# Every loop of the five engines' programs written out as straight-line code

## The chip, the cores and the metric

The kernel runs on one core of a Trainium2 chip. The metric is the device time of one execution in microseconds (us); lower is better. The kernel before takes 1512.36 us, the median of three runs (1511.91 to 1512.64).

## The reference, cut to what matters

The input is `x` (32 x 64 tokens of 256 numbers) with a context of the same shape. Two cross-attention layers with 16 heads of 128 come first, then an MLP, then a third attention with 16 small heads, then another MLP. All is float32.

```python
def _cross_attention(q_in, kv_in, wq, bq, wk, bk, wv, bv, wo, bo, bias_k, bias_v):
    qh = (q_in @ wq + bq).reshape(b, q_len, H, K)          # H, K = 16, 128
    kh = (kv_in @ wk + bk).reshape(b, t, H, K)             # and one bias key per head
    vh = (kv_in @ wv + bv).reshape(b, t, H, K)
    weights = softmax(einsum('bqhk,bthk->bhqt', qh, kh) / sqrt(K))
    return einsum('bhqt,bthk->bqhk', weights, vh).reshape(b, q_len, H * K) @ wo + bo

x = x + cross_attention(layer_norm(x), ctx)    # layer 1
x = x + cross_attention(layer_norm(x), ctx)    # layer 2
x = x + gelu(layer_norm(x) @ w_fc1 + b_fc1) @ w_fc2 + b_fc2
# then: 16 heads of 16, keys from ctx (masked) and x, residual, RMS norm, and a second MLP
```

## The kernel before, in words

Each of the five engines has its own program, and semaphores tie them together. Float32 products are made of three products of split numbers (a high part and a low part), which the helper `three` issues (lines 168 to 170). So almost all matmul rows carry these three line numbers.

**The two cross-attention layers** fill most of the time. A layer is 32 units: 8 pairs of heads by 4 groups of 512 tokens. In one slot an engine works on the front of one unit (queries, keys, values, logits) and on the back of the unit before it (probabilities by values, and the output projection with `WHI` and `CHI`). The logits of a unit are the matmuls of line 413. `slots` (line 241) calls `slot` once for the first unit, then runs a loop (`Fori`, line 248) whose body holds 8 slots and that runs three times, and then writes the last 8 slots out. Around that stands the loop over the two layers (line 466 on PE, 538 on ACT, 660 on DVE, 306 on POOL). POOL has an inner loop of its own over pairs of weights (line 309), and SP one over the weight loads (line 273).

**The two MLPs** (`mlp`, tags m0 and m1) go over four groups of tokens. The first group is written out and the other three are one loop (`groups`, line 686).

**The third attention** is 64 steps in a software pipeline, two for each batch. `steps` writes the first 9 out, then runs a loop of four steps a turn, 13 turns (line 1024), and then writes the rest. A step on PE is four logits matmuls (line 1066), one mask matmul (1070), four transposes (1080) and eight products with the values (1092); every other step has one more transpose (1101).

An induction variable of `Fori` lives in a register. Addresses are given as `bass.ds(2 * m, 2)`, and the wait values, `e.wait_ge(q_done, 2 * n + h + 1)` say, are worked out by register instructions on the engine that waits. At its end a loop has one register addition and one compare and branch on each engine. A `Block` ends with a barrier, and its beginning is an unconditional branch.

Of the kernel before, what the change touches and what calls it, by code (L numbers as in the profile page):

```python
# [20 lines left out]
NL = 2  # L21
# [23 lines left out]
def program(nc, x, ctx_in, mask, wall, vech, vecm, b_fc2, qw, kw, vw, ow, out_b, w1, w2, b2, out):  # L45
    es = ExitStack()
    with es:
# [139 lines left out]
        with ExitStack() as ph:  # L187
# [54 lines left out]
            def slots(e, L, slot):  # L242

                slot(L, L * UNITS, 0, L * HP, None, False)
                with e.Fori(0, UNITS // OLD - 1) as i:
                    for u in range(OLD):
                        slot(L, L * UNITS + i * OLD + u + 1, u + 1, L * HP + i * 2 + (u + 1) // G, i * 2 + u // G, False)  # L250
                i = UNITS // OLD - 1
                for u in range(OLD):
                    slot(L, L * UNITS + i * OLD + u + 1, u + 1,
                         L * HP + i * 2 + (u + 1) // G if u < OLD - 1 else None, i * 2 + u // G, True)

            with nc.Block() as block:
                @block.sync
                def _(e):
                    def load(m, a):
                        e.dma_start(W[a][:, :, :, :], wall[m].rearrange("j (c p) n -> p j c n", p=P)).then_inc(w_in[a], 16)  # L260

                    ct, xt = (v.rearrange("(t p) d -> p t d", p=P) for v in (ctx_in, x))
                    for g in range(G):
                        ts = slice(g * GT, (g + 1) * GT)
                        if g >= 2:

                            e.wait_ge(ctx_turned, (g - 1) * DC)
                        e.dma_start(cin[g % 2][:, :, :], ct[:, ts, :]).then_inc(ctx_in_g[g], 16)
                        e.dma_start(X[:, ts, :], xt[:, ts, :]).then_inc(x_in[g], 16)
                        if g == 0:  # L270
                            load(0, 0)
                    load(1, 1)
                    with e.Fori(1, SETS // 2) as i:
                        for a in range(2):
                            m = i * 2

                            e.wait_ge(w_split, m + a - 1)
                            e.wait_ge(bw_done, m + a - 1)
                            load(m + a, a)

                @block.gpsimd
                def _(e):
                    e.memset(one, 1.0).then_inc(ident_one, 1)
                    e.wait_ge(ident_one, 1)
                    e.affine_select(out=ident[:, :], in_=one, compare_op=ALU.is_equal, fill=0.0, base=0,
                                    pattern=[[-1, P]], channel_multiplier=1).then_inc(ident_done, 1)
                    e.memset(EA[:, :, :], 0.0)
                    e.memset(EB[:, :, :], 0.0).then_inc(e_made, 1)
                    e.memset(PTB[:, :, :], 1.0)
                    e.memset(PRT[:, :, :], 0.0).then_inc(zeros_set, 1)  # L290

                    def split(m, a):

                        e.wait_ge(w_hi, m + 1)
                        for j in range(4):
                            i = e.tensor_tensor(WLO[a][:, j, :, :], W[a][:, j, :, :],  # L296
                                                WHI[a][:, j, :, :].bitcast(F32), ALU.subtract)
                        e.tensor_tensor(E2[a][:, :, :], EA[:, bass.ds(2 * m, 2), :], EB[:, bass.ds(2 * m, 2), :],
                                        ALU.subtract)
                        e.tensor_copy(PB[a][:, :, :], PH[:, :, bass.ds(2 * m, 2)]).then_inc(w_split, 1)  # L300

                    e.wait_ge(e_made, 3)
                    split(0, 0)
                    for g in range(G - 1):
                        norm_lo(e, norm, 0, g)
                    with e.Fori(0, NL) as L:
                        norm_lo(e, norm, L, G - 1)
                        split(L * HP + 1, 1)
                        with e.Fori(0, HP // 2 - 1) as i:
                            for a in range(2):  # L310
                                split(L * HP + i * 2 + 2 + a, a)
                        split(L * HP + HP, 0)
                        for g in range(G - 1):
                            norm_lo(e, norm, L + 1, g)

                @block.tensor
                def _(e):
# [145 lines left out]
                            norm_turn(e, norm, 0, k, PROJ[2:])  # L463

                    e.wait_ge(ctx_lo, G * DC)
                    with e.Fori(0, NL) as L:
                        slots(e, L, slot)

                @block.scalar
                def _(e):  # L470
# [64 lines left out]
                    norm_sqrt(e, norm, 0, 2)  # L535
                    norm_scale(e, norm, 0, 1, PROJ[2:])
                    norm_scale(e, norm, 0, 2, PROJ[2:])
                    with e.Fori(0, NL) as L:
                        slots(e, L, slot)

                @block.vector
                def _(e):
                    logit = logits[:, :, 0:GT * KEYS].rearrange("p h (t k) -> p h t k", k=KEYS)

                    def slot(L, n, at, pair, hp, last):
# [8 lines left out]
                        if back:  # L554
# [2 lines left out]
                            e.wait_ge(sm_done, n)  # L557
                            e.reciprocal(ri[:, :], sm[:, :]).then_inc(ri_done, 1)
                            e.wait_ge(ri_done, n)
                            e.tensor_tensor(PTB[:, gb * GT:(gb + 1) * GT, bass.ds(2 * hp, 2)].rearrange("p t h -> p h t"),  # L560
                                            ex[:, :, S].rearrange("p (h t) -> p h t", h=2),
                                            ri[:, :].rearrange("p (h t) -> p h t", h=2), ALU.mult)
                            e.tensor_tensor(PR[:, :, :], ex[:, :, 0:S], ri[:, :].unsqueeze(2).to_broadcast([P, 2 * GT, S]),
# [9 lines left out]
                        if bridge and gb == 0:  # L573
                            e.wait_ge(bw_turned, L + 1)
                            e.tensor_copy(BW[:, :], PROJ[3][0:32, 0:D]).then_inc(bw_out, 1)

                            e.tensor_copy(CUR[:, :], PM[:, bass.ds((L + 1) * LNP, 4)]).then_inc(cur_set, 1)
                        if norm_now is not None and front:

                            e.wait_ge(x_settled, 2 * n if back else 2 * n + 2)  # L580
# [76 lines left out]
                            round_set(0, 0)  # L657
                    e.wait_ge(x_in[G - 1], 16)
                    e.memset(mx[:, :], 0.0).then_inc(x_settled, 2)
                    with e.Fori(0, NL) as L:  # L660
                        e.memset(BWT[:, :, :], 0.0).then_inc(bwt_sum, 1)
                        e.wait_ge(bwt_sum, L * BWTN + 1)
                        e.tensor_copy(BWT[:, :, H + 1], PM[:, bass.ds(L * LNP + 4, 2)]).then_inc(bwt_sum, 1)
                        slots(e, L, slot)


# [3 lines left out]
        def mlp(tag, norm, k, b1, w, ready, b2d, func, dst, more):  # L670
# [3 lines left out]
            with ExitStack() as ph:  # L674
# [8 lines left out]
                def groups(e, body, tail=None):  # L683

                    body(0, True)
                    with e.Fori(1, G) as g:
                        body(g, False)
                    if tail is not None:
                        tail()

                with nc.Block() as block:  # L691
# [13 lines left out]
                    def _(e):  # L705
                        def body(g, first):
                            for j in range(FC):
# [8 lines left out]
                                    more["gpsimd"](e)  # L716
                                if j == 3:

                                    xs = X[:, bass.ds(g * GT, GT), :]
                                    e.tensor_tensor(xs, xs, b2b[:, :].unsqueeze(1).to_broadcast([P, GT, D]),  # L720
                                                    ALU.add).then_inc(b2_added, 1)

# [22 lines left out]
                    def _(e):  # L745
                        def add(g):

                            e.wait_ge(b2_added, g + 1)
                            e.wait_ge(down_used, FC * (g + 1))  # L749
                            for j in range(2):  # L750
                                xs = X[:, bass.ds(g * GT + 2 * j, 2), :]
                                e.tensor_tensor(xs, xs, bank[3 + j][:, :].rearrange("p (t n) -> p t n", n=256),  # L752
                                                ALU.add).then_inc(y_added, 1)

# [21 lines left out]
                    def _(e):  # L776
# [12 lines left out]
                            i.then_inc(down_used, 1)  # L789

                        def body(g, first):
                            toks = bass.ds(g * GTOK, GTOK)
# [68 lines left out]
        with ExitStack() as l1:  # L861
# [136 lines left out]
            with ExitStack() as ph:  # L998
# [20 lines left out]
                def steps(e, slot):  # L1019

                    for s in range(LR + 1):
                        slot(s, s, 0)
                    rest = (STEPS - LR - 1) // 4
                    with e.Fori(0, rest) as i:
                        for r in range(LR + 1, LR + 5):
                            slot(i * 4 + r, r, i * 2)
                    for s in range(LR + 1 + rest * 4, STEPS + LR):
                        slot(s, s, 0)
# [4 lines left out]
                with nc.Block() as block:  # L1033
                    @block.gpsimd
                    def _(e):
                        def slot(s, r, b0):
                            if runs(r, 0):
# [5 lines left out]
                                q = QL[:, r % 2, bass.ds((b0 + other) * S, S)]  # L1043
                                e.tensor_tensor(QE[r % 4][:, :, :], q.unsqueeze(1).to_broadcast([P, GH, S]),
                                                HM[:, :].unsqueeze(2).to_broadcast([P, GH, S]),
                                                ALU.mult).then_inc(qe_set, 1)
                            if runs(r, LR) and (r - LR) % 2 == 0:
                                b = b0 + (r - LR) // 2
                                e.wait_ge(ao_hi, b + 1)
                                toks = bass.ds(b * S, S)  # L1050
# [88 lines left out]
                    def _(e):  # L1139
                        def slot(s, r, b0):  # L1140
# [23 lines left out]
                            if runs(r, LA) and (r - LA) % 2 == 0:  # L1164
                                b, c = b0 + (r - LA) // 2, (r - LA) // 2 % 2
                                e.wait_ge(at_out, 2 * b + 2)
                                e.tensor_copy(SRC_HI[:, 1, :, bass.ds(b * S, S)], AT[c][:, :, :]).then_inc(ao_hi, 1)


                        e.wait_ge(ow_in, 16)  # L1170
# [160 lines left out]
```

## Time and profile before

| | |
|---|---|
| median of three runs | 1512.36 us |
| the three runs | 1511.91 to 1512.64 us |
| span of the profiled execution, first to last instruction | 1511.0 us |
| TensorE (PE) matmuls busy | 1426.2 us, 94% |
| weight loads (PEld) | 1274.8 us, 84% |
| VectorE (DVE) | 895.5 us, 59% |
| ScalarE (ACT) | 626.1 us, 41% |
| GpSimd (POOL) | 340.7 us, 23% |
| mean granted TensorE clock | 0.966 |
| instructions | 29462 |

The profile has no device time of the profiled execution beside its span; the median of the runs lies 1.36 us above that span, which is what surrounds the first and the last instruction. A row that names a releaser says what ended the idle time before an instruction; "issue" there means that the engine waited for nothing that the profile shows. Rows with a q behind the engine are its sequencer's (register instructions, branches, waits). PE and PEld are issued by one sequencer.

### The profile page before, as it was taken

What the parts mean: (1) busy time and instruction counts of PE and PEld (TensorE: products, weight loads), DVE (VectorE), ACT (ScalarE), POOL (GpSimd) and SP (SyncE); (2) the same over time, 40 slices, a digit from 0 to 9 for tenths busy, and PEclk for the clock granted to TensorE, in tenths of its full rate; (3) what the DMA queues carried; (4) which work ended last, traced back from release to release, by engine and by line L of the source; (5) the groups of instructions that cost most, each with busy time, mean ns of one, the idle gap of its engine ahead of it and who ended that gap; (6) DMA issues with size and microseconds to landing.
All of it is one profiled execution on the core that took longest, in us unless ns stands there. A gap on an engine that the chain in (4) does not pass through costs nothing. (4 is left out here: it accounts for less than half of the span.)

```text
span 1511.0 us, 29462 instructions
## 1 busy us (share of the span) xinstructions
PE 1426.2 (94%) x11575; PEld 1274.8 (84%) x11575; DVE 895.5 (59%) x1929; ACT 626.1 (41%) x1053; POOL 340.7 (23%) x322
## 2 busy tenths in 40 slices
PE   4999999999999899999999999998898999997898
PEld 3899899899998778988998999986787888887787
DVE  6566567566666646666665666665523377776422
ACT  4533344334333543433343344343422336666521
POOL 4201101101011111101101011020754035555654
PEclk8999999999999979999999999997899999999899
DMA  5000000000000000000000000000000000001000
GB/s 169 29 29 1 30 5 25 30 1 29 29 2 29 1 30 1 29 29 1 29 1 30 29 1 29 29 1 1 25 0 8 0 1 1 0 0 60 4 28 28
DMA packets 28991, 30.42 MB, mean 20 GB/s; under 512 B 651, under 2 KB 28883, under 8 KB 28883
## 3 DMA queue, kind: packets, MB, share of 16 engines
q1 hardware_dynamic: 28658, 28.72, 6.0%
q8 instruction: 88, 1.44, 0.4%
q14 instruction: 19, 0.16, 0.0%
q10 hardware_dynamic: 226, 0.10, 0.0%
HBM read 26.72 MB, written 2.10 MB: 19 GB/s over the span
## 5 line engine op out<-in xcount | busy, mean ns | idle before, releaser
L296 POOL TENSOR_TENSOR WLO<-W,WHI 128x512 fp32r<-128x512 f32 x68 | 85.1, 1283 | 793.5 <-DVE WHI L623 793.5
L168 PE MATMUL bank<-SRC_HI,WHI 128*128 128x512 f32 (+1 forms) x576 | 233.4, 405 | 18.5 <-issue 14.6
L169 PE MATMUL bank<-SRC_LO,WHI 128*128 128x512 f32 (+1 forms) x576 | 231.9, 403 | 0.0
L170 PE MATMUL bank<-SRC_HI,WLO 128*128 128x512 f32 (+1 forms) x576 | 231.5, 402 | 0.0
L570 DVE STREAM_TRANSPOSE PRT<-PR 32x256 f32<-32x256 f32 x512 | 223.3, 436 | 8.4
L591 DVE TENSOR_TENSOR CLO<-bank,CHI 128x512 fp32r<-128x512 f32 x128 | 88.2, 691 | 159.3 <-ACT CHI L502 159.1
L478 ACT ACTIVATE QT<-bank,PB 128x512 f32<-128x512 f32 x128 | 88.2, 690 | 209.2 <-PE bank L170 209.2
L168 PE MATMUL bank<-WHI,CHI 128*128 128x256 f32 x512 | 155.2, 303 | 0.0
L168 PE MATMUL bank<-WHI,SRC_HI 128*128 128x256 f32 x512 | 149.4, 292 | 0.0
L168 PEld LDWEIGHTS bank<-SRC_HI,WHI 128*128 128x128 f32 x576 | 111.2, 193 | 42.7 <-issue 15.4
L170 PE MATMUL bank<-WHI,CLO 128*128 128x256 f32 x512 | 145.6, 284 | 0.0
L169 PE MATMUL bank<-WLO,CHI 128*128 128x256 f32 x512 | 145.6, 284 | 0.0
L169 PE MATMUL bank<-WLO,SRC_HI 128*128 128x256 f32 x512 | 143.9, 281 | 0.0
L170 PE MATMUL bank<-WHI,SRC_LO 128*128 128x256 f32 x512 | 143.9, 281 | 0.0
L617 DVE TENSOR_TENSOR X<-X,bank 128x512 f32<-128x512 f32 x128 | 88.0, 688 | 85.9 <-PE bank L170 85.9
L385 PE MATMUL bank<-PRT,V 128*128 128x128 f32 x1024 | 128.3, 280 | 7.8 <-issue 6.0
L170 PEld LDWEIGHTS bank<-SRC_HI,WLO 128*128 128x128 f32 x576 | 110.8, 192 | 26.9
L169 PEld LDWEIGHTS bank<-SRC_LO,WHI 128*128 128x128 f32 x576 | 111.4, 193 | 22.6
L385 PEld LDWEIGHTS bank<-PRT,V 128*128 128x128 f32 x1024 | 122.8, 196 | 8.7 <-issue 6.5
L482 ACT ACTIVATE KT<-bank,PB 128x512 f32<-128x512 f32 x128 | 88.4, 691 | 91.7 <-PE bank L170 91.7
L486 ACT ACTIVATE V<-bank 128x512 f32<-128x512 f32 x128 | 76.5, 597 | 97.6 <-PE bank L170 97.2
L168 PEld LDWEIGHTS bank<-WHI,CHI 128*128 128x128 f32 x512 | 98.3, 192 | 17.0 <-issue 13.2
(182 smaller groups left out, 2976.5 us busy)
## 6 DMA issues: line engine op xcount, KB each, us to landing
W<-in_wall SPq DMA_DIRECT2D x18, 1024.0 KB, 5.6
V<-in_ctx SPq DMA_DIRECT2D x4, 512.0 KB, 5.5
X<-in_x SPq DMA_DIRECT2D x4, 512.0 KB, 6.5
mlp_w<-in_w SPq DMA_DIRECT2D x2, 1024.0 KB, 7.4
out<-X SPq DMA_DIRECT2D x4, 512.0 KB, 3.0
W<-in_qw SPq DMA_DIRECT2D x1, 256.0 KB, 3.9
W<-in_kw SPq DMA_DIRECT2D x1, 256.0 KB, 4.1
W<-in_vw SPq DMA_DIRECT2D x1, 256.0 KB, 4.9
```

Source lines behind the costliest of these rows:

```text
L168: e.matmul(dst, a_hi, b_hi, start=start, stop=False, **kw)
L169: e.matmul(dst, a_hi, b_lo, start=False, stop=False, **kw)
L170: return e.matmul(dst, a_lo, b_hi, start=False, stop=stop, **kw)
L296: i = e.tensor_tensor(WLO[a][:, j, :, :], W[a][:, j, :, :], WHI[a][:, j, :, :].bitcast(F32), ALU.subtract)
L385: i = e.matmul(bank[3 + h][:, p * P:(p + 1) * P], V[(at - 1) % 2][:, p, h * K:(h + 1) * K], PRT[:, h * GT + p, :], start=True, stop=True)
L478: e.activation(QT[:, h, :], PROJ[h][:, :], ACT.Identity, bias=PB[a][:, 0, h:h + 1]).then_inc(q_out, 1)
L482: e.activation(KT[:, h, :, 0:S], PROJ[2 + h][:, :].rearrange("p (q k) -> p q k", k=S), ACT.Identity, bias=PB[a][:, 1, h:h + 1]).then_inc(k ...
L486: e.activation(V[at % 2][:, 2 * j:2 * j + 2, :], PROJ[j][:, :].rearrange("p (t n) -> p t n", n=256), ACT.Copy).then_inc(v_out, 1)
L570: i = e.transpose(PRT[b * S + z:b * S + z + 32, :, b * S + y:b * S + y + 32], PR[b * S + y:b * S + y + 32, :, z:z + 32])
L591: e.tensor_tensor(CLO[:, h, :], bank[3 + h][:, :], CHI[:, h, :].bitcast(F32), ALU.subtract).then_inc(c_lo, 1)
L617: e.tensor_tensor(xs, xs, bank[3 + j][:, :].rearrange("p (t n) -> p t n", n=256), ALU.add).then_inc(x_settled, 1)
```

## The change

Every `with e.Fori(a, b) as i:` becomes `for i in range(a, b):`, which the program builder runs, so that the body stands in the program once for each turn. Addresses by `bass.ds` become plain slices. The wait values become constants, since they are computed while the program is built. No matmul, activation, vector operation, DMA or semaphore is added, left out or put elsewhere in its engine's order.

```diff
 def slots(e, L, slot):
-    with e.Fori(0, UNITS // OLD - 1) as i:
+    for i in range(0, UNITS // OLD - 1):
         for u in range(OLD):
             slot(L, ...)
...
-    with e.Fori(1, SETS // 2) as i:               # SP, weight loads
+    for i in range(1, SETS // 2):
...
-    with e.Fori(0, NL) as L:                      # PE, ACT, DVE, POOL
+    for L in range(0, NL):
         slots(e, L, slot)
...
-    with e.Fori(0, HP // 2 - 1) as i:             # POOL, weight splits
+    for i in range(0, HP // 2 - 1):
...
-    e.tensor_copy(PB[a][:, :, :], PH[:, :, bass.ds(2 * m, 2)]).then_inc(w_split, 1)
+    e.tensor_copy(PB[a][:, :, :], PH[:, :, slice(2 * m, 2 * m + 2)]).then_inc(w_split, 1)
...
 def groups(e, body, tail=None):                   # both MLPs
     body(0, True)
-    with e.Fori(1, G) as g:
+    for g in range(1, G):
         body(g, False)
...
 def steps(e, slot):                               # third attention
-    with e.Fori(0, rest) as i:
+    for i in range(0, rest):
         for r in range(LR + 1, LR + 5):
             slot(i * 4 + r, r, i * 2)
```

On PE, at the end of the eight-slot body of the cross-attention, the program before has this (the products with `CHI` and `CLO` are the output projection of one unit; the branch leads back to the top of the body, where the products with `SRC_HI` of the next unit begin):

```order
L168 MATMUL bank<-WHI,CHI 128x256
L169 MATMUL bank<-WLO,CHI 128x256
L170 MATMUL bank<-WHI,CLO 128x256
L248 REGISTER_ALU
L248 COMPARE_AND_BRANCH
```

and the changed program has this at the same place:

```order
L168 MATMUL bank<-WHI,CHI 128x256
L169 MATMUL bank<-WLO,CHI 128x256
L170 MATMUL bank<-WHI,CLO 128x256
L168 MATMUL bank<-SRC_HI,WHI 128x512
L169 MATMUL bank<-SRC_LO,WHI 128x512
L170 MATMUL bank<-SRC_HI,WLO 128x512
```

The register instruction and the branch are gone, and the next unit's first matmul stands right behind.

On PE in the third attention, the last step of the body before (an ISA row is a register instruction that makes an address or a wait value):

```order
L1061 REGISTER_ALU
L1066 ISA
L1066 MATMUL bank<-KL,QE 128x128 x4
L1070 ISA
L1070 MATMUL bank<-MA,ONE 128x4x64
L1080 MATMUL bank<-ident,XN 128x128 x4
L1092 MATMUL bank<-VS,HT 64x17 x8
L1098 ISA
L1100 REGISTER_ALU
L1101 MATMUL logits<-ident,AN 128x128
L1024 REGISTER_ALU
L1024 COMPARE_AND_BRANCH
```

and one such step of the changed program:

```order
L1066 MATMUL bank<-KL,QE 128x128 x4
L1070 MATMUL bank<-MA,ONE 128x4x64
L1080 MATMUL bank<-ident,XN 128x128 x4
L1092 MATMUL bank<-VS,HT 64x17 x8
L1101 MATMUL logits<-ident,AN 128x128
```

The matmuls keep their order; seven register and branch rows go.

## Rows read from the trace of the kernel before

**Rows 1.** The page's first part, all engines: busy us, share, instructions
```profile
PE 1426.2 (94%) x11575; PEld 1274.8 (84%) x11575; DVE 895.5 (59%) x1929; ACT 626.1 (41%) x1053; POOL 340.7 (23%) x322
```

**Rows 2.** Waits, whole span: us in total, times, longest us
```profile
PE bank L168 <- issue: 14.6, 4, 3.7
PE bank L168 <- DVE X L752: 1.5, 6, 0.5
```

**Rows 3.** Instructions of line 248, duration ns min/median/max, first and last start us
```profile
L248 PEldq COMPARE_BRANCH  x6: 83/5410/5536, 162.6 to 919.2; - x6
```

**Rows 4.** Timeline of PE around the first turn: start us, us, what, idle before
```profile
168.39 0.49 PE L168 MATMUL bank<-SRC_HI,WHI 128*128 128x512 f32 x1 [3.67 <-issue]
169.18 0.39 PE L168 MATMUL bank<-SRC_HI,WHI 128*128 128x512 f32 x1
...
170.15 0.63 PE L168 MATMUL bank<-SRC_HI,WHI 128*128 128x512 f32 x1
```

**Rows 5.** Windows: stretch, us, busy (x) of PE, PEld, DVE, ACT, POOL; PEclk; DMA; GB/s
```profile
169.54:172.95 3.41, 3.41 (x10) 2.63 (x9) 2.59 (x5) 0.69 (x1) 0.67 (x1) 0.50 0.00 0
290.34:295.83 5.49, 5.49 (x13) 4.33 (x14) 3.77 (x7) 0.69 (x1) 1.54 (x2) 0.50 0.01 3
681.53:684.95 3.42, 3.42 (x10) 2.65 (x9) 3.20 (x6) 0.69 (x1) 0.05 (x1) 0.50 0.00 0
```

**Rows 6.** Timeline of PE, first logits matmuls of four units
```profile
160.56 0.34 PE L413 MATMUL logits<-KT,QT 128*64 128x65 f32 x4
180.38 0.34 PE L413 MATMUL logits<-KT,QT 128*64 128x65 f32 x4
405.49 0.33 PE L413 MATMUL logits<-KT,QT 128*64 128x65 f32 x3
419.84 0.28 PE L413 MATMUL logits<-KT,QT 128*64 128x65 f32 x2
```

**Rows 7.** Windows, the unit of the last two rows above
```profile
405.50:419.80 14.30, 14.30 (x121) 13.04 (x120) 10.56 (x21) 5.20 (x8) 2.74 (x3) 1.00 0.24 74
```

**Rows 8.** Instructions of line 1024, third attention's loop
```profile
L1024 PEldq COMPARE_BRANCH  x13: 76/208/232, 1257.0 to 1368.4; - x13
```

**Rows 9.** Timeline of PEld, line 1092, inside the loop; turns at 1284.9 and 1294.2
```profile
1284.52 0.55 PEld L1092 LDWEIGHTS bank<-VS,HT 128*64 128x64 f32 x16 [0.17 <-issue]
1287.11 0.55 PEld L1092 LDWEIGHTS bank<-VS,HT 128*64 128x64 f32 x16 [0.17 <-issue]
...
1293.80 0.55 PEld L1092 LDWEIGHTS bank<-VS,HT 128*64 128x64 f32 x16 [0.17 <-issue]
1296.39 0.55 PEld L1092 LDWEIGHTS bank<-VS,HT 128*64 128x64 f32 x16 [0.17 <-issue]
```

**Rows 10.** Timeline of PEld, line 1092, in the straight steps behind the loop
```profile
1370.32 0.55 PEld L1092 LDWEIGHTS bank<-VS,HT 128*64 128x64 f32 x16 [0.17 <-issue]
1372.53 0.55 PEld L1092 LDWEIGHTS bank<-VS,HT 128*64 128x64 f32 x16 [0.17 <-issue]
1374.80 0.55 PEld L1092 LDWEIGHTS bank<-VS,HT 128*64 128x64 f32 x16 [0.17 <-issue]
```

**Rows 11.** Instructions of line 686, the MLPs' loops
```profile
L686 PEldq COMPARE_BRANCH  x6: 76/210/233, 1105.2 to 1499.2; - x6
```

**Rows 12.** Instructions of line 466, the loop over layers on PE
```profile
L466 PEldq COMPARE_BRANCH  x2: 74/1754/3433, 543.5 to 1055.1; - x2
```

**Rows 13.** Waits on DVE, 545 to 551 us
```profile
DVE BWT L661 <- issue: 2.4, 1, 2.4
```

**Rows 14.** DMA queues, 168 to 288 us, one turn of the body: packets, MB
```profile
q8 instruction: 10, 0.16, 0.5%
```

**Rows 15.** DMA queues, 410 to 530 us, eight units written out
```profile
q8 instruction: 7, 0.11, 0.5%
```

**Rows 16.** DMA queues, 1258 to 1370 us, third attention's loop, the only instruction queue
```profile
q14 instruction: 1, 0.01, 0.0%
```

**Rows 17.** Windows, one turn of the third attention's loop
```profile
1294.24:1303.52 9.28, 9.22 (x126) 8.21 (x122) 7.25 (x19) 6.36 (x15) 4.96 (x6) 1.00 0.00 0
```

More of the change, by code:

```diff
@@ L297, in split @@
                                                 WHI[a][:, j, :, :].bitcast(F32), ALU.subtract)
-                        e.tensor_tensor(E2[a][:, :, :], EA[:, bass.ds(2 * m, 2), :], EB[:, bass.ds(2 * m, 2), :],
+                        e.tensor_tensor(E2[a][:, :, :], EA[:, slice(2 * m, 2 * m + 2), :], EB[:, slice(2 * m, 2 * m + 2), :],
                                         ALU.subtract)
-                        e.tensor_copy(PB[a][:, :, :], PH[:, :, bass.ds(2 * m, 2)]).then_inc(w_split, 1)
+                        e.tensor_copy(PB[a][:, :, :], PH[:, :, slice(2 * m, 2 * m + 2)]).then_inc(w_split, 1)
                     e.wait_ge(e_made, 3)
@@ L465, in _ @@
                     e.wait_ge(ctx_lo, G * DC)
-                    with e.Fori(0, NL) as L:
+                    for L in range(0, NL):
                         slots(e, L, slot)
@@ L537, in _ @@
                     norm_scale(e, norm, 0, 2, PROJ[2:])
-                    with e.Fori(0, NL) as L:
+                    for L in range(0, NL):
                         slots(e, L, slot)
@@ L559, in slot @@
                             e.wait_ge(ri_done, n)
-                            e.tensor_tensor(PTB[:, gb * GT:(gb + 1) * GT, bass.ds(2 * hp, 2)].rearrange("p t h -> p h t"),
+                            e.tensor_tensor(PTB[:, gb * GT:(gb + 1) * GT, slice(2 * hp, 2 * hp + 2)].rearrange("p t h -> p h t"),
                                             ex[:, :, S].rearrange("p (h t) -> p h t", h=2),
@@ L575, in slot @@
                             e.tensor_copy(BW[:, :], PROJ[3][0:32, 0:D]).then_inc(bw_out, 1)
-                            e.tensor_copy(CUR[:, :], PM[:, bass.ds((L + 1) * LNP, 4)]).then_inc(cur_set, 1)
+                            e.tensor_copy(CUR[:, :], PM[:, slice((L + 1) * LNP, (L + 1) * LNP + 4)]).then_inc(cur_set, 1)
                         if norm_now is not None and front:
@@ L659, in _ @@
                     e.memset(mx[:, :], 0.0).then_inc(x_settled, 2)
-                    with e.Fori(0, NL) as L:
+                    for L in range(0, NL):
                         e.memset(BWT[:, :, :], 0.0).then_inc(bwt_sum, 1)
                         e.wait_ge(bwt_sum, L * BWTN + 1)
-                        e.tensor_copy(BWT[:, :, H + 1], PM[:, bass.ds(L * LNP + 4, 2)]).then_inc(bwt_sum, 1)
+                        e.tensor_copy(BWT[:, :, H + 1], PM[:, slice(L * LNP + 4, L * LNP + 4 + 2)]).then_inc(bwt_sum, 1)
                         slots(e, L, slot)
@@ L717, in body @@
                                 if j == 3:
-                                    xs = X[:, bass.ds(g * GT, GT), :]
+                                    xs = X[:, slice(g * GT, g * GT + GT), :]
                                     e.tensor_tensor(xs, xs, b2b[:, :].unsqueeze(1).to_broadcast([P, GT, D]),
@@ L750, in add @@
                             for j in range(2):
-                                xs = X[:, bass.ds(g * GT + 2 * j, 2), :]
+                                xs = X[:, slice(g * GT + 2 * j, g * GT + 2 * j + 2), :]
                                 e.tensor_tensor(xs, xs, bank[3 + j][:, :].rearrange("p (t n) -> p t n", n=256),
@@ L791, in body @@
                         def body(g, first):
-                            toks = bass.ds(g * GTOK, GTOK)
+                            toks = slice(g * GTOK, g * GTOK + GTOK)
                             for j in range(FC):
@@ L1042, in slot @@
                                 other = r // 2 + (1 if r // 2 % 2 == 0 else -1)
-                                q = QL[:, r % 2, bass.ds((b0 + other) * S, S)]
+                                q = QL[:, r % 2, slice((b0 + other) * S, (b0 + other) * S + S)]
                                 e.tensor_tensor(QE[r % 4][:, :, :], q.unsqueeze(1).to_broadcast([P, GH, S]),
@@ L1049, in slot @@
                                 e.wait_ge(ao_hi, b + 1)
-                                toks = bass.ds(b * S, S)
+                                toks = slice(b * S, b * S + S)
                                 e.tensor_tensor(SRC_LO[:, 1, :, toks], AT[(r - LR) // 2 % 2][:, :, :],
@@ L1166, in slot @@
                                 e.wait_ge(at_out, 2 * b + 2)
-                                e.tensor_copy(SRC_HI[:, 1, :, bass.ds(b * S, S)], AT[c][:, :, :]).then_inc(ao_hi, 1)
+                                e.tensor_copy(SRC_HI[:, 1, :, slice(b * S, b * S + S)], AT[c][:, :, :]).then_inc(ao_hi, 1)
                         e.wait_ge(ow_in, 16)
```

## The prediction

> **What bounds the kernel now.** The page's first part comes first: PE is busy for 1426.2 of 1511.0 us and no other engine for more than 895.5 [rows 1]. So a microsecond counts if PE would otherwise have worked in it. The waits of PE come next, and among them one kind has no releaser at all: line 168 waits for "issue" four times, 14.6 us together [rows 2]. The reader should then ask which instruction of PE's sequencer stands there. Line 248, the branch at the end of the eight-slot body, has six executions, with a median of 5410 ns and a smallest of 83 ns [rows 3]. The body runs three times in each of two layers, so four branches are taken and two fall through: four long ones and four waits. In the timeline the first turn shows 3.67 us without a matmul, and then something that a list of waits cannot show: the 512-column matmul takes 0.39 us right behind the gap and 0.63 us from 170.15 on [rows 4]. The granted clock there is 0.50 [rows 5], the lower of the two levels, 1.2 GHz, after PE had stood still.
>
> **Part 1: the four turns of the cross-attention loop.** The gaps: 14.6 us. The low clock behind them: three windows of 3.41, 5.49 and 3.42 us with PE busy all through, at clock 0.50 [rows 5], and a fourth behind the fourth turn as long as the third, 15.7 us in all, of which half, 7.9 us, is work that the full clock would have saved. Together 22.5 us. A second reading: the unit across the first turn lasts 180.38 - 160.56 = 19.82 us from logits to logits, and the unit at the same place of the schedule, between the third body and the eight slots written out behind it, 419.84 - 405.49 = 14.35 us [rows 6]. In that unit the clock is 1.00 and PE is busy throughout [rows 7]. The difference, 5.47 us, is the 3.67 us gap and the 1.7 us of clock behind it. I take 22.5 us. What is late next? Where no branch is taken PE meets no other wait in its unit, so nothing stands behind the gap to take its place. The other engines are busy for 10.56 us or less of such a unit [rows 7]; their cover stays.
>
> Why a turn costs so much is seen in the instruction queue: 10 packets of 16 KB in one turn of the body [rows 14] and 7 in a stretch of equal length and equal work that is written out [rows 15]. The jump back asks again for code that the core no longer holds. The Trainium skill says so too (Runtime: NRT & Kernel Launch, Instruction fetch mechanics): a taken branch whose target is outside the loaded pages has to wait for a fetch. By that rule and the rows alike, these four go.
>
> **Part 2: the loop over layers.** Its taken branch holds PE's sequencer for 3433 ns [rows 12], but PE works off queued matmuls meanwhile: the four waits of rows 2 are used up by the inner turns. DVE stands idle for 2.4 us at the same place [rows 13]. I cost this part at nothing. The cover is PE's own queue and DVE's slack; at most it gives the 2.4 us of DVE.
>
> **Part 3: the third attention.** A branch takes 208 ns here [rows 8], and no 16 KB packet is fetched in the 112 us of the loop [rows 16]. Yet it shows on PE: from one step's products with the values to the next it is 1287.11 - 1284.52 = 2.59 us across a turn, and 1296.39 - 1293.80 = 2.59 us again [rows 9], while the steps written out behind the loop alternate between 2.21 and 2.27 us [rows 10]. That is 0.32 us a turn: the branch, and the register instructions after it that make the first addresses while PE's queue has run dry. Twelve turns are taken: 12 x 0.32 = 3.8 us. The ends are 0, if something else fills the place, and 12 x 0.38 = 4.6 us against the shorter step. I take 3.8, since the straight steps do the same work.
>
> A rule of the Trainium skill gives another price here (Advanced Engine Details and Errata, Control Flow Timing): about 108 ns for a compare and branch. Our trace has 208 ns for the branch and 0.32 us for the turn. An estimate by the page is 12 x 0.108 = 1.3 us for this part in place of 3.8, and the whole would come out 2.5 us higher.
>
> **Part 4: the MLPs.** The branch takes 210 ns [rows 11], behind queued matmuls; the only waits of PE near it are six for DVE's addition into X, 1.5 us in all [rows 2]. That dependency stays; DVE reaches it perhaps 50 ns sooner without register instructions. I take 0.3 us, between 0 and 1.5.
>
> **Part 5: register instructions elsewhere.** Hundreds of them go on every engine. In the units PE waits for nobody [rows 7], so they are worth nothing there. At the bridges between layers PE waits on a chain over DVE and ACT; some tens of ns at each of a handful of waits. I take 0.3 us, between 0 and 2.
>
> **What it may cost.** The third attention and the MLPs now need code fetched where they turned within held code. In the units a packet lasts 120 / 7 = 17 us [rows 15], which at 241 matmuls and weight loads in 14.3 us [rows 7] is 288 of them. A turn of the third attention has 248 [rows 17]: about 10 packets for 12 turns, and, by an estimate of one packet each, 4 or 5 for the four repeated MLP groups (two in each MLP): 15. Straight code is fetched ahead in the units without any gap on PE, so I cost this at nothing, with a bound under the rivals.
>
> **The sum.** 22.5 + 3.8 + 0.3 + 0.3 = 26.9 us off. The span goes from 1511.0 to 1484.1 us, and with the 1.36 us around it (the median stands so far above the span) the time is 1485.5 us. The low-clock windows come in steps of about 3.4 us and begin where PE has idled; everything behind 165 us moves, so the other places where the clock falls, the bridges and the changes from phase to phase, may each win or lose part of a step, half of which is time. I allow 4 us either way.
>
> **Rivals.** *The stall goes but the low clock stays.* If those windows came from something other than the gaps, power say, only 14.6 + 3.8 + 0.6 = 19.0 us go: 1493.4 us. For it: the clock falls up to 1.2 us after the gap has ended. Against: in the units with no branch it never falls. *The turn moves instead of going.* If each new packet in straight code cost what a turn costs now, 3.65 us of gap and 2 us of clock, only where code was held before, 5.6 in all, 15 x 5.6 = 84 us would come on and 26.9 go: 1569 us, slower. It decides from 26.9 / 15 = 1.8 us a packet. For it: the third attention works through its code half as fast again as the units (248 instructions in 9.28 us against 241 in 14.3) [rows 7, 17], with shorter steps to hide a fetch in. Against: the units fetch straight code all the time and show no gap [rows 7, 15]. The skill (same section as above) holds such crossings mostly hidden. *Half effect.* PE's gap shrinks but the unit behind it stumbles over something that was late under its cover (DVE's transposes at that place, 10.6 us of work in 14.35), about 1 to 1.5 us a turn, and the third attention is held by DVE at 2.3 us a step: some 7 us less gain, 1492 us. *It gives more.* The register instructions on DVE and ACT shorten the bridges by 2 us and two low-clock steps vanish: 1481 us. That the change doesn't do what it says is excluded by the order of PE's instructions, which has no such branch left.
>
> **How the numbers follow.** My forecast with its few us about it has 0.72, more gain 0.06, half effect 0.08, low clock that stays 0.08, slower by fetches 0.04, and 0.02 for next to nothing. A measurement of this kernel tells 0.2%, 3 us, from no change, so all but the last two are faster: 0.94, 0.02, 0.04. The range goes from 1480.0, the larger ends of parts 3 to 5 with some luck of the clock, to 1492.5, the smaller ends with bad luck and the half effect; it leaves out the slower rival and the low clock that stays.
>
> **What would show it.** No branch of line 248, no wait of PE's line 168 for "issue" of 3.6 us; units without a branch's gap, of 14.35 us at that place, all through both layers; granted clock 1.00 from about 36 to 500 us; steps of 2.21 and 2.27 us throughout the third attention, with some 10 packets on the instruction queue in it. I am wrong if PE has gaps at packets in straight code, if the clock falls in the middle of the units without a gap, or if some step of the third attention still lasts 2.6 us.

## The result, and the profile after

The changed kernel takes 1484.97 us, the median of four runs (1484.72 to 1485.71), against 1512.46 us for the kernel before in runs beside it: a ratio of 0.9817, with a 95% interval of 0.9803 to 0.9831. The forecast was 1485.5 us. The profiled execution has a span of 1483.9 us, 27.1 us less than before.

The page's first parts, of the changed kernel; they answer to [rows 1]:

```profile
span 1483.9 us, 27446 instructions
...
PE 1415.3 (95%) x11575; PEld 1268.7 (85%) x11575; DVE 897.6 (60%) x1929; ACT 623.5 (42%) x1053; POOL 339.5 (23%) x322
...
PEclk8999999999999989999999999997999999998899
...
q8 instruction: 92, 1.51, 0.4%
```

The counts of real work are those of before, and 2016 instructions are gone, all of them the sequencers'. PE is busy for 10.9 us less with the same 11575 matmuls. 8.1 us of that is the clock's (worked out in the table under the third attention's loop); most of the rest lies in the third attention, where the busy time falls by 3.1 us at clock 1.00 (the step rows below). The instruction queue q8 carried 92 packets; before there were 88. That is about what the prediction's counts give: four turns no longer fetch three packets each again, and 15 packets of new code come on.

The waits of PE in line 168, which answer to [rows 2], of the changed kernel (us in total, times, longest):

```profile
PE bank L168 <- PEq L1199: 4.0, 1, 4.0
PE bank L168 <- PEq L256: 3.9, 1, 3.9
PE bank L168 <- DVE Y L1244: 2.3, 1, 2.3
PE bank L168 <- DVE SRC_LO L933: 1.7, 1, 1.7
PE bank L168 <- PEq L1033: 1.7, 1, 1.7
PE bank L168 <- DVE X L752: 0.6, 1, 0.6
```

The four waits for "issue", 14.6 us, have gone, and of the six for DVE's addition into X one is left. The unit at the first turn lasted 19.82 us before [rows 6]. Its first logits matmul and that of the next unit are now at:

```profile
160.97 0.34 PE L413 MATMUL logits<-KT,QT 128*64 128x65 f32 x4
...
175.36 0.34 PE L413 MATMUL logits<-KT,QT 128*64 128x65 f32 x4
```

It lasts 14.39 us. The third attention, where [rows 9] had 2.59 us across a turn, is even at 2.21 and 2.27 us:

```profile
1254.30 0.55 PEld L1092 LDWEIGHTS bank<-VS,HT 128*64 128x64 f32 x16 [0.17 <-issue]
1256.51 0.55 PEld L1092 LDWEIGHTS bank<-VS,HT 128*64 128x64 f32 x16 [0.17 <-issue]
1258.79 0.55 PEld L1092 LDWEIGHTS bank<-VS,HT 128*64 128x64 f32 x16 [0.17 <-issue]
```

The gain of this part can be read in one view: from the first step's products with the values to the last step's, the same 1811 matmuls on PE, at clock 1.00 in both kernels (before, then changed; the columns are explained below):

```profile
1236.58:1377.43 140.85, 140.05 (x1811) 124.93 (x1811) 110.25 (x275) 97.23 (x214) 70.66 (x86) 1.00 0.00 1
1209.52:1346.62 137.10, 136.98 (x1811) 124.07 (x1811) 110.01 (x275) 95.04 (x214) 70.59 (x87) 1.00 0.01 2
```

That is 3.75 us. And the DMA queues over what was its loop, 1230 to 1338 us, now show code being fetched, where [rows 16] had no q8:

```profile
q8 instruction: 11, 0.18, 0.6%
```

Where the 27.1 us went is best read stage by stage. The windows view takes a list of stretches; here both kernels are cut at the same events (first logits of each layer, last logits of each layer, first matmul of each phase). The columns are the stretch, its length, the busy time of PE, PEld, DVE, ACT and POOL with their instructions, PEclk, DMA share, GB/s. The kernel before:

```profile
45.70:515.60 469.90, 461.74 (x3791) 416.84 (x3790) 302.64 (x633) 189.72 (x294) 48.61 (x52) 0.99 0.06 19
515.60:558.30 42.70, 35.81 (x199) 28.56 (x198) 20.01 (x60) 16.23 (x26) 5.21 (x4) 0.76 0.01 2
558.30:1027.30 469.00, 460.78 (x3793) 416.06 (x3792) 302.72 (x634) 189.77 (x294) 48.57 (x52) 0.99 0.06 19
1027.30:1063.40 36.10, 25.29 (x133) 18.87 (x132) 15.93 (x43) 11.25 (x16) 5.11 (x4) 0.68 0.00 0
...
1228.80:1381.50 152.70, 149.71 (x1888) 133.68 (x1888) 117.83 (x290) 101.72 (x225) 78.91 (x96) 0.98 0.00 1
1381.50:1412.00 30.50, 17.92 (x120) 17.10 (x121) 16.26 (x24) 18.10 (x43) 20.31 (x11) 0.84 0.23 74
```

The changed kernel:

```profile
46.30:504.20 457.90, 457.15 (x3793) 413.66 (x3792) 303.34 (x634) 189.62 (x294) 48.45 (x52) 1.00 0.06 20
504.20:545.50 41.30, 34.41 (x197) 27.79 (x196) 20.33 (x60) 16.27 (x25) 5.18 (x4) 0.79 0.00 1
545.50:1003.50 458.00, 457.26 (x3792) 413.74 (x3791) 303.29 (x634) 189.62 (x294) 48.47 (x52) 1.00 0.06 20
1003.50:1038.10 34.60, 24.23 (x133) 18.03 (x133) 15.88 (x43) 11.25 (x17) 5.11 (x4) 0.75 0.00 1
...
1203.20:1350.90 147.70, 144.53 (x1889) 130.44 (x1889) 117.54 (x290) 99.45 (x225) 78.35 (x96) 0.99 0.01 2
1350.90:1384.40 33.50, 21.24 (x120) 20.35 (x120) 14.90 (x24) 18.07 (x43) 20.21 (x11) 0.75 0.26 67
```

The two layers give 12.0 and 11.0 us, the turns. The bridge and the end of the second layer give 1.4 and 1.5 us, both with less PE busy time at a higher clock. The third attention gives 5.0 us: 3.75 for the turns, and most of the rest because its first steps were not at the low clock this time. The change of phase behind it takes 3.0 us back: PE is busy for 3.3 us more with the same 120 matmuls, at clock 0.75 instead of 0.84. The stretches not shown add up to about +0.8 us: the start, the first MLP with what lies behind it, and the last MLP.

### The profile page after: what moved, and what is told of

Its sections match the earlier page's. It is cut to its first block and busy times, and to the rows that moved or that the text cites. A ratio compares the mean times of both kernels' runs of the same rounds, so it can differ in the third digit from the quotient of the medians.

```text
span 1483.9 us, 27446 instructions
## 1 busy us (share of the span) xinstructions
PE 1415.3 (95%) x11575; PEld 1268.7 (85%) x11575; DVE 897.6 (60%) x1929; ACT 623.5 (42%) x1053; POOL 339.5 (23%) x322
## 5 line engine op out<-in xcount | busy, mean ns | idle before, releaser
L168 PE MATMUL bank<-SRC_HI,WHI 128*128 128x512 f32 x576 | 230.4, 400 | 3.9 <-PEq L256 3.9
L169 PE MATMUL bank<-SRC_LO,WHI 128*128 128x512 f32 x576 | 229.4, 398 | 0.0
L170 PE MATMUL bank<-SRC_HI,WLO 128*128 128x512 f32 x576 | 229.0, 398 | 0.0
```

Source lines behind the costliest of these rows:

```text
L168: e.matmul(dst, a_hi, b_hi, start=start, stop=False, **kw)
L169: e.matmul(dst, a_hi, b_lo, start=False, stop=False, **kw)
L170: return e.matmul(dst, a_lo, b_hi, start=False, stop=stop, **kw)
```

## The experiments

Times of kernels are medians. Each ratio is to the kernel before in runs beside it, with its 95% interval. All kernels but the changed one itself are made from the kernel before with one helper, at the end of the file so that line numbers keep:

```python
def turns(e, line, start, end):
    if STRAIGHT:                  # a condition on line and e.engine, given with each run
        yield from range(start, end)
        return
    with e.Fori(start, end) as i:
        yield i
```

Every `with e.Fori(a, b) as i:` reads `for i in turns(e, line, a, b):`. Where a loop is kept, its branch has the helper's line (1338 or 1339) in the profile.

### One loop of one engine

```diff
-    if STRAIGHT:
+    if line == 248 and e.engine == mybir.EngineType.PE:
```

> Only PE's loop of line 248 (three turns of eight slots) is written out; the loop over layers, the MLP and third-attention loops and all loops of the other engines stay. Theory (PE fetches its code again at a taken branch of that loop, and idles into the low clock): the four gaps of 3.6 us and the low clock behind them go, 22.5 us less than before, about 1490 us; units across the turn 14.35 us. Rival (the gain of the change is spread over register instructions and loops of all engines): less than half of it here, 1500 us or more.

Measured: 1488.15 us (four runs) against 1510.75 us (21 runs of before), ratio 0.9843 (0.9828 to 0.9858), 22.6 us less; the interval goes from 21.5 to 26.0 us. The units have 14.35 to 14.39 us at all four places, and line 168's wait for "issue" is gone. The forecast of 22.5 us for this part is met, and it comes from a loop of PE alone. What the trace leaves is the rest: steps of 2.57 to 2.61 us at the turns of the third attention, and the six waits for DVE's addition.

```profile
PE bank L168 <- DVE X L752: 1.3, 6, 0.3
```

### The other four engines, and PE alone

```diff
-    if STRAIGHT:
+    if e.engine != mybir.EngineType.PE:      # x2
+    if e.engine == mybir.EngineType.PE:      # x3
```

> All loops of DVE, ACT, POOL and SP are written out, PE keeps every loop. Theory: PE's gaps and low-clock windows all stay, the time is that of before within 1 us (1511 to 1513 us). Rival (DVE's turns and register instructions matter): 1509 us or less.

> All loops of PE are written out, the other engines keep theirs. Theory: practically the whole gain, 1485 to 1487 us, since the other engines' turns are off the path; at most 1.5 us above the full change, at the bridges between layers where PE waits on DVE and ACT. Rival: the gain of the full change minus the part of the others, 1490 us or more.

Measured: with every engine but PE written out 1513.36 us (ten runs), ratio 1.0009 (0.9995 to 1.0022), no gain (0.4 us above the range that I expected, 1511 to 1513). With PE alone written out 1487.21 us (four runs), ratio 0.9839 (0.9824 to 0.9854), which overlaps the interval of the full change. The first kernel's trace still has the old row:

```profile
PE bank L168 <- issue: 13.9, 4, 3.6
```

So nearly all of the gain is PE's. Turns and register instructions of DVE, ACT, POOL and SP are worth nothing that the times can show here. The traces show about 1 us of theirs, in PE's waits for DVE's addition in the MLPs: the first row is of the kernel with all but PE written out, the second of PE alone:

```profile
PE bank L168 <- DVE X L752: 0.5, 1, 0.5
PE bank L168 <- DVE X L752: 1.7, 6, 0.3
```

Five of the six waits go when DVE's program is written out and stay when only PE's is. That is the effect that part 4 of the prediction put at 0.3 us; it is 1.0 to 1.2 us in these traces. Whether the 2.2 us between the medians of PE alone and the full change are real stays open: their intervals overlap.

### The third attention's loop alone

```diff
-    if STRAIGHT:
+    if line == 1024:
```

> Only the third attention's loop (line 1024) is written out, on every engine. Theory: 12 turns of 0.32 us, 3.8 us less than before (1508.6 us), every step 2.21 or 2.27 us. By the 108 ns a page gives for a branch it would be 1.3 us. Rival (new code must be fetched and holds PE): no gain or a loss.

Measured: 1509.85 us (eleven runs) against 1510.75 us (21 runs), ratio 0.999 (0.998 to 1.0). That is 0 to 3 us less, and the forecast 3.8 us lies just outside. The medians mislead here: one execution of before differs from the next by up to 9 us (1505.85 to 1514.82), and the eleven runs had less clock (median 0.965 against 0.968). Among runs with the same mean granted clock, from 0.964 to 0.968 (one to six runs of each kernel), the kernel with this loop written out is on average 2.2 to 5.0 us shorter. The steps tell it without the clock. The stretch of 140.85 us above reads

```profile
1232.61:1369.70 137.09, 136.97 (x1811) 124.05 (x1810) 110.23 (x275) 95.17 (x214) 70.63 (x87) 1.00 0.01 2
```

with steps of 2.21 and 2.27 us at all 12 turns. The same trace bears on the spread. Its first cross-attention turn has a gap of 3.32 us and no low clock behind it (its timeline of PE, and then its window from 168 to 172 us, with PEclk third from the end); the third, of 3.31 us, has one:

```profile
168.19 0.50 PE L168 MATMUL bank<-SRC_HI,WHI 128*128 128x512 f32 x1 [3.32 <-issue]
```

```profile
168.00:172.00 4.00, 3.81 (x16) 3.12 (x17) 3.89 (x8) 1.38 (x2) 0.00 (x0) 1.00 0.02 4
```

What the clock does behind a gap is thus not fixed for a kernel. To take it out, I add up in each trace the time in which PE was busy while the clock stood at 0.50, and take half of it off the span:

| kernel | span | PE busy at 0.50 | span less half of it | against before |
|---|---|---|---|---|
| before | 1511.0 | 77.2 | 1472.4 | |
| all but PE written out | 1512.8 | 81.4 | 1472.2 | -0.2 |
| third attention's loop alone | 1504.3 | 72.1 | 1468.3 | -4.1 |
| PE's line 248 alone | 1487.2 | 61.3 | 1456.6 | -15.8 |
| PE alone | 1485.0 | 61.1 | 1454.5 | -17.9 |
| the full change | 1483.9 | 61.0 | 1453.4 | -19.0 |

These are single executions, in us, to be read to about 1 us: in the third attention's kernel the four gaps were also 0.9 us shorter (13.7 against 14.6), which is in its 4.1. The full change's 19.0 us is what the prediction's terms without the clock come to (14.6 + 3.8 + 0.3 + 0.3), and the other 8.1 us (half of 77.2 - 61.0) are the clock's. Of these, 7.9 are the four windows behind the gaps; at all other places together PE was busy at the low clock for 61.5 us before and 61.0 after.

### The loop over layers put back

```diff
-    if STRAIGHT:
+    if line not in (306, 466, 538, 660):
```

> The changed kernel with the loop over the two layers put back on PE, ACT, DVE and POOL; everything inside it stays written out. One turn is taken, over a body of some 8000 PE instructions. Theory: PE's branch waits about 3.4 us for code behind queued matmuls and DVE stands idle 2.4 us, both hidden, so the time is that of the full change, 1485 us, within 1.5 us. Rival (every taken branch back to code no longer held costs PE 5.6 us): 1490.5 us.

Measured: 1485.55 us (four runs), ratio 0.9842 (0.9818 to 0.9865), the time of the full change. The branch waits as long as before, and the time does not show it:

```profile
L1338 PEldq COMPARE_BRANCH  x2: 83/1798/3512, 530.0 to 1030.8; - x2
```

Here a long taken branch costs nothing, since PE's queue holds slow work for as long: in the 3.5 us of this branch PE is busy all through, with 13 matmuls at clock 0.50.

### Gaps without a branch

```diff
+    if n % 32 in (8, 16):                       # DVE, behind its addition into X
+        for c in range(4):                      # x7; range(7) in x9
+            e.wait_ge(held, 4 * (2 * L + n % 32 // 8 - 1) + c)
+            e.tensor_copy(scr, ident broadcast to 128x512).then_inc(held, 1)
...
+    if n % 32 in (9, 17):                       # PE, ahead of the queries
+        e.wait_ge(held, 4 * (2 * L + n % 32 // 8))
```

In x9 the 4 in both waits is a 7 too. The copies write a tile that nobody reads.

> The changed kernel, no loop anywhere, but at the four places of the former turns DVE makes four idle copies behind its addition into X and PE waits for the last before the next unit's queries: four gaps on PE of 2.5 to 4 us without any branch. Theory (the low clock follows the idle time, whatever its cause): low-clock windows of one or two steps of 3.4 us behind most of the gaps, and each lengthened unit is longer by its gap and half of its low-clock time; with gaps of 3.5 us the time is 1484.97 + 14 + 7 = 1506 us, and at least 10 us above the changed kernel. Rival (the low clock came with the jump or the code fetch): only the gaps, clock 1.00 behind them, 1499 us.

> As the kernel with four gaps, but with seven copies of 0.46 us in place of four, so that PE's gaps grow from 2.50 us to about 3.9 us, as long as those before the change. Theory (whether the low clock comes depends on how long PE stood still, and 2.5 us is mostly too short): low clock behind at least three of the four gaps, 1484.97 + 15.5 + 5 to 9 us = 1505 to 1509 us. Rival (the low clock is a matter of the jump or of fetching code, and the one window at 2.5 us was an accident): clock 1.00 behind all four, 1500.5 us.

Measured with four copies: 1495.93 us (four runs), ratio to before 0.9916 (0.9888 to 0.9945), 11.0 us over the full change's median. The wait of PE, and then windows behind each of the four gaps:

```profile
PE bank L168 <- DVE scr L625: 10.0, 4, 2.5
```

```profile
168.00:180.00 12.00, 12.00 (x102) 10.74 (x101) 8.04 (x16) 5.16 (x8) 5.41 (x6) 1.00 0.01 1
287.00:289.84 2.84, 2.84 (x7) 2.26 (x8) 2.71 (x8) 0.00 (x0) 0.00 (x0) 0.50 0.00 0
674.00:686.00 12.00, 12.00 (x103) 10.75 (x102) 8.03 (x16) 5.15 (x8) 5.41 (x6) 1.00 0.01 1
793.00:805.00 12.00, 12.00 (x100) 10.71 (x101) 8.04 (x16) 5.15 (x8) 5.41 (x6) 1.00 0.01 1
```

The gaps are of 2.5 us, 10.0 us in all, and only one of the four was followed by the low clock. My expectation of "most of the gaps" was wrong, and with it the 1506 us. One of the four runs took 1500.01 us at a lower mean clock (0.967 against 0.972 or 0.973), so this kernel too has executions with more of the low clock.

Measured with seven copies: 1510.54 us (ten runs), ratio to before 0.9991 (0.9981 to 1.0001): the whole gain is given back without a single branch. The gaps are of 3.9 us, and the clock is low behind all four (the same two views):

```profile
PE bank L168 <- DVE scr L625: 15.6, 4, 3.9
```

```profile
169.91:173.33 3.42, 3.42 (x10) 2.65 (x9) 3.30 (x8) 0.69 (x1) 0.00 (x0) 0.50 0.00 0
291.07:296.21 5.14, 5.14 (x12) 4.07 (x13) 4.94 (x13) 0.69 (x1) 0.00 (x0) 0.50 0.01 2
681.91:685.33 3.42, 3.42 (x10) 2.65 (x9) 3.26 (x9) 0.69 (x1) 0.00 (x0) 0.50 0.02 5
804.79:808.21 3.42, 3.42 (x9) 2.64 (x8) 3.30 (x9) 0.69 (x1) 0.00 (x0) 0.50 0.00 0
```

This is the picture of [rows 5]. The low clock comes behind PE's idle time without a jump and without a refetch of code. Half of the 15.4 us is 7.7; with the 15.6 us of gaps that makes 23.3 us, and the span of this execution, 1507.5 us, is 23.6 us over that of the full change (1483.9).

### How large a body can turn cheaply

The changed kernel, but on PE the third attention stays a loop with a body of 24 steps, which runs twice. The body is then made larger by issuing the same transposes again into the same place:

```diff
-    if STRAIGHT:
+    if not (line == 1024 and e.engine == mybir.EngineType.PE):
...
-    for i in turns(e, 1024, 0, rest):
-        for r in range(LR + 1, LR + 5):
-            slot(i * 4 + r, r, i * 2)
+    for i in turns(e, 1024, 0, 2):
+        for r in range(LR + 1, LR + 25):
+            slot(i * 24 + r, r, i * 12)
...
-    for j in range(JP):                      # transposes of a step
+    for j in list(range(JP)) * 3:            # x8; * 2 in x10; [0, 1, 0, 1, 2, 3] in x11
```

> The changed kernel, but on PE alone the third attention is a loop whose body holds 24 steps and runs twice: one taken branch over a body of about 1600 instructions, six or seven packets of 16 KB (the cross-attention body had about 2010, some eight packets). If PE holds that much, the turn costs 0.3 us and no packet is fetched in the second turn; if it holds less, the step across the turn is 3 us or more longer and six packets are fetched a second time.

> As the 24-step loop, but every step's four transposes (line 1080) are issued three times over, into the same place, so that the body grows to about 1990 instructions, the size of the cross-attention body; the time is longer by the added work. If size alone decides, this turn shows what line 248 showed: packets fetched again and a gap of about 3 us on PE behind the branch. Rival (something else in the cross-attention loop makes the turn long): a turn of 0.3 us as with the short body.

> The 24-step loop on PE with the transposes issued twice, a body of about 1770 instructions, between the 1577 that turned in 0.24 us without a packet and the 1961 that were fetched again and held the branch for 3.37 us. If what counts is whether the whole body still lies in what PE holds, it is one or the other with nothing between: a branch of about 0.24 us and no new packet, or of about 3.4 us and two packets more than straight code needs. I expect the held case, since it is a packet less than the cross-attention body.

> The 24-step loop on PE with six transposes a step in place of four (two of them twice), a body of about 1673 instructions, 6.5 packets, between 1577 (held) and 1769 (fetched again). No forecast which; the two outcomes are a branch of about 0.24 us with no packet in the second turn, or one of about 3.4 us with the packets fetched again. Anything between (a branch of 1 to 3 us) would speak against the account that the whole window is lost at once.

One execution of each. The rows of the branch (the smallest is the one not taken, the largest the one taken), in order of the body's size:

```profile
L1339 PEldq COMPARE_BRANCH  x2: 76/156/237, 1275.7 to 1329.8; - x2
```

```profile
L1339 PEldq COMPARE_BRANCH  x2: 76/152/229, 1281.7 to 1341.0; - x2
```

```profile
L1339 PEldq COMPARE_BRANCH  x2: 83/1725/3367, 1289.0 to 1358.4; - x2
```

```profile
L1339 PEldq COMPARE_BRANCH  x2: 83/1728/3373, 1302.4 to 1382.2; - x2
```

| PE instructions from branch to branch | kernel | taken branch | packets of 16 KB in the second turn | time |
|---|---|---|---|---|
| 1577 | 24 steps | 237 ns | 0 | 1483.95 us |
| 1673 | two transposes more a step | 229 ns | 0 | 1497.63 us |
| 1769 | transposes twice | 3367 ns | 9 | 1515.98 us |
| 1961 | transposes three times | 3373 ns | 10 | 1545.74 us |
| 2014 to 2017 | cross-attention, before | 5410 ns | 10 [rows 14] | |

The counts take in matmuls, weight loads and 161 of the sequencer's own instructions. The times hold the extra transposes and are not to be compared with each other. Between 1673 and 1769 it changes at once: 96 instructions more, and all of the body is fetched again where none of it was. I had expected the body of 1769 to be held; that was wrong. Each size has one execution and one place of the body in the program; whether that place matters was not tried. At 1769 PE is idle for 3.2 us at the turn, and the low clock follows (the waits of PE, and a window behind the gap):

```profile
PE bank L1067 <- POOL QE L1045: 6.3, 2, 3.2
```

```profile
1292.80:1296.10 3.30, 3.30 (x15) 3.24 (x16) 0.97 (x2) 0.00 (x0) 0.12 (x1) 0.50 0.02 5
```

The profile puts this gap down to POOL's QE, the semaphore that the next matmul looks at (the other of the two waits is the start of the third attention, which every kernel here has). With the branch over it from 1289.0 on for 3367 ns, it is the branch's: where such a row names an engine that was done long before, look for the sequencer.

The cross-attention's branch took 2 us more than the 3.4 us of a body of about the same size. Size does not explain that: the body of the loop over layers holds over 7500 matmuls and weight loads, and its branch took 3.43 us [rows 12]. What the DMA engines did meanwhile may. Windows over four taken branches, the first turn of line 248 and the loop over layers (before), then bodies of 1769 and 1961:

```profile
162.60:168.00 5.40, 2.12 (x19) 1.92 (x17) 4.40 (x11) 0.64 (x1) 0.00 (x0) 1.00 0.55 181
543.50:546.90 3.40, 3.40 (x13) 2.75 (x14) 0.69 (x1) 0.00 (x0) 0.00 (x0) 0.50 0.02 5
1289.00:1292.40 3.40, 0.57 (x13) 0.35 (x9) 0.95 (x4) 1.65 (x5) 1.93 (x3) 1.00 0.02 5
1302.40:1305.70 3.30, 0.53 (x11) 0.31 (x7) 0.64 (x3) 1.60 (x5) 1.88 (x3) 1.00 0.02 5
```

At each turn of line 248 a weight transfer of 1 MB was under way; it had begun 0.7 us before the branch. From 162.6 to 165.5 us it kept the DMA engines busy for 96.3% of the time, and no other queue moved a packet:

```profile
q1 hardware_dynamic: 910, 0.93, 96.3%
```

The first packet of code came at 165.55 us, as the transfer ended, 2.9 us after the start of the branch. In the 12 turns with such a transfer, in three traces, that took 2.6 to 3.1 us; in the seven long branches without one, in seven traces, 0.9 to 1.3 us. From that packet to the end of the branch it was 2.3 to 2.6 us in all 19. So some 2 us of each turn go with the transfer. No run moved the transfer away from the branch, so that it is the cause is likely and not shown.

## Why the prediction was right

**The turns of line 248** were to give 22.5 us. The single loop of one engine gave 22.6 us, the two layers' stretches 12.0 and 11.0. The reading of the profile (four waits without a releaser, and a branch with a median of 5410 ns beside a smallest of 83 ns) named the cause, and the windows gave the clock's third of the price. Confirmed in each half: gap without low clock in the third attention's run, low clock without branch in the run with seven copies.

**The fetch as the cause.** The prediction argued it from ten packets against seven, and from the Trainium skill (Runtime: NRT & Kernel Launch, Instruction fetch mechanics). The series of body sizes shows it: no packet, no gap. The same section speaks of a window of two pages, though, a page being 256 instructions, and gives PE's store as 2048 instructions; on PE here a body of 1673 instructions still turned without a packet, and one of 1769 did not. Neither figure agrees as a limit for a body that turns cheaply, and the measurement decides. What the prediction did not see is that the price of a turn depends on more than the jump: some 2 us of each 5.4 us branch go with the weight transfer that ran at the same time. Its sum is not touched, since it took the gaps as they were measured.

**The loop over layers** was costed at nothing, and put back it costs nothing.

**The third attention**: 12 turns of 0.32 us, 3.8 us. Each turn of 2.59 us has become 2.27 us, and the stretch from the first step to the last is 3.75 us shorter with the full change and 3.76 us with this loop alone. The times of that kernel show 0 to 3 us less, with a worse draw of the clock. The Trainium skill's 108 ns for a compare and branch (Advanced Engine Details and Errata, Control Flow Timing) was too low a price for a turn here: the branch took 208 ns in the median [rows 8] and the steps show 0.32 us.

**The MLPs** were to give 0.3 us because DVE reaches its addition into X sooner. The mechanism is right and the size too small: the waits fell from 1.5 to 0.6 us, and by 1.0 us when all engines but PE were written out.

**New code to fetch.** I counted 10 packets in the third attention and found 11; none of them stopped PE, so the slower rival has no case. The half effect has none either: PE's steps went at 2.21 and 2.27 us. Nor has the low clock that stays: the clock was 1.00 over both layers.

**What was only lucky.** The prediction took the clock behind the four gaps as a fixed 7.9 us. In other executions the same turns can cost more or less: one gap of 3.32 us had none. It also gave 0.3 us to register instructions at the bridges, which no run shows. The bridges gained 1.4 and 1.5 us, the first by the clock alone, the second by 1.1 us of clock and 0.4 us less idle time, and a bridge wait that fell with the full change (PE for DVE's XN, line 128, 11.0 to 10.6 us) was as short with the third attention's loop alone and longer, 11.6, with all engines but PE written out. The change of phase behind the third attention lost 3.0 us, also by the clock. That the allowance of 4 us either way came out at 0.5 is chance: the terms without the clock were exact to the tenth in this pair of traces only as a sum, and all the places besides the four gaps cancelled to 0.2 us of clock. The base was lucky too: against the median of the 21 later runs of the kernel before, 1510.75 us, the change takes off 25.8 us and not 27.5.

## What to carry to other kernels

Look for branches whose duration has two values: a taken one of several microseconds beside one of 80 ns says that the body is larger than what the engine holds, and the price is the gap plus the low clock that PE falls into. By the sizes tried here a loop's body on PE should stay under about 1670 instructions (matmuls, weight loads and the sequencer's own all count), or be written out; loops on engines off the path can stay. Look also at what large transfer starts just before such a branch. Write out only what a turn costs something for: here one loop of one engine gave 22.6 of 27.5 us.

## What the runs showed of the hardware that was not expected

- What PE's sequencer holds has a sharp edge: 1673 instructions, no packet; 1769, nine packets and a branch of 3.37 us. With 2014 to 2017 instructions the branch took 5.4 us, two microseconds more than with 1961. The first packet of code came 2.6 to 3.1 us after the start of each of the 12 branches with a 1 MB weight transfer under way, and 0.9 to 1.3 us after that of the seven without.
- Written-out code cost nothing to fetch at any pace met here, 11 packets of 16 KB in 108 us included, and the 3.51 us of the layer loop's long taken branch were hidden.
- Whether the clock falls behind a gap goes with the gap's length but not with it alone: at 2.5 us one of four, at 3.2 us both (the bodies of 1769 and 1961), at 3.3 to 3.7 us eleven of twelve (the turns of three traces), at 3.9 us all four. Runs of one kernel, 1505.85 us (clock 0.973) to 1514.82 us (clock 0.964) for the kernel before, are consistent with such draws; that was not tried by itself.
